# First-layer value products issued in three bursts of four, four and five token tiles in a two-layer cross-attention kernel

## What is computed

```python
q = _split_heads(hidden_states @ w_q, HEADS)
k = _split_heads(text @ w_k, HEADS)
v = _split_heads(text @ w_v, HEADS)
out_text = _merge_heads(_sdpa(q, k, v))            # softmax(q k^T / sqrt(dh)) v, 1593 text tokens
out_ip = _merge_heads(_sdpa(q, k_ip, v_ip, mask=mask_ip))   # 8 further tokens
out = (out_text + IP_SCALE * out_ip) @ w_out + b_out + residual
```

## Time and profile before

| What | Value |
|---|---|
| Median of 3 runs | 1550.36 us |
| The profiled execution: its own time | 1552.15 us |
| The profiled execution: span of the trace | 1550.2 us |
| TensorE busy | 1456.7 us (94%) |
| VectorE busy | 1119.9 us (72%) |
| ScalarE busy | 1060.8 us (68%) |
| First layer's products (line 1083), first and last start | 230.3 us, 636.4 us |
| First layer's products: MATMUL records, busy | 2080, 175.5 us |

### The profile page before, as it was taken

How to read it: one execution, slowest core, us unless ns; L and a number is a source line. 1 busy time by engine, 2 the same in 40 slices (tenths; PEclk the granted TensorE clock), 3 DMA queues, 4 the chain that set the end, 5 groups by cost and what they waited for, 6 DMA issues and landing times. The chain is left out here.

```text
span 1550.2 us, 32737 instructions
## 1 busy us (share of the span) xinstructions
PE 1456.7 (94%) x12886; PEld 911.9 (59%) x12886; DVE 1119.9 (72%) x1572; ACT 1060.8 (68%) x1962; POOL 188.8 (12%) x363
## 2 busy tenths in 40 slices
PE   6797959999999999999999999999999999999995
PEld 4454513333333333477777777777777777777774
DVE  5777768887787877876767777777777777777625
ACT  2454538877877877767767777777777777777752
POOL 4653300000101101000010000000000000000000
PEclk9899959999999999899999999999999999999996
DMA  5266851221221212110011101100011001100000
GB/s 158 75 161 174 226 115 48 53 51 40 58 54 47 66 40 51 42 26 23 17 26 30 29 19 26 26 23 20 23 26 26 22 18 27 26 23 16 7 1 17
DMA packets 82902, 75.89 MB, mean 49 GB/s; under 512 B 28608, under 2 KB 70964, under 8 KB 82756
## 3 DMA queue, kind: packets, MB, share of 16 engines
q1 hardware_dynamic: 82756, 73.88, 18.3%
HBM read 47.73 MB, written 26.09 MB: 48 GB/s over the span
## 5 line engine op out<-in xcount | busy, mean ns | idle before, releaser
L1364 DVE TENSOR_TENSOR whole<-late,whole 128x1024 f16<-128x1024 f32 (+1 forms) x280 | 320.1, 1143 | 99.3 <-ACT whole L1223 96.2
L1349 DVE TENSOR_REDUCE mx<-ps_y 128x2 f32<-128x800 f32 (+2 forms) x227 | 223.9, 986 | 106.1 <-PE ps_y L1030 105.4
L1107 PE MATMUL ps_v<-eh,whole 128*128 128x269 f16 x1040 | 293.1, 282 | 0.0
L1107 PE MATMUL ps_n<-eh,whole 128*128 128x269 f16 x1040 | 291.6, 280 | 0.0
L1223 ACT CAST whole<-late 128x1024 f16<-128x1024 f32 (+1 forms) x280 | 275.6, 984 | 8.9
L1109 PE MATMUL ps_v<-el,whole 128*128 128x269 f16 x960 | 269.1, 280 | 0.0
L1110 PE MATMUL ps_v<-eh,whole 128*128 128x269 f16 x960 | 269.1, 280 | 0.0
L1110 PE MATMUL ps_n<-eh,whole 128*128 128x269 f16 x960 | 268.2, 279 | 0.0
L1109 PE MATMUL ps_n<-el,whole 128*128 128x269 f16 x960 | 268.1, 279 | 0.0
L1349 DVE TENSOR_REDUCE mx<-ps_x 128x2 f32<-128x800 f32 (+2 forms) x198 | 195.3, 987 | 82.0 <-PE ps_x L1030 81.1
L1349 DVE TENSOR_REDUCE mx<-ps_t 128x2 f32<-128x800 f32 (+2 forms) x215 | 211.4, 983 | 32.8 <-PE ps_t L1030 31.9
(11 more groups left out here) (433 smaller groups left out, 2072.9 us busy)
## 6 DMA issues: line engine op xcount, KB each, us to landing
e<-in_ctx SPq DMA_DIRECT2D x4, 1536.0 KB
kb<-k_parts SPq DMA_DIRECT2D x80, 74.9 KB
kb<-k_parts SPq DMA_DIRECT2D x80, 74.7 KB
k_parts<-kp SPq DMA_DIRECT2D x12, 400.0 KB
vb<-v_cols SPq DMA_DIRECT2D x40, 117.0 KB, 2.1
v_cols<-late SPq DMA_DIRECT2D x4, 1040.0 KB, 11.7
late<-v_cols SPq DMA_DIRECT2D x40, 104.0 KB, 2.0
qb<-q_parts SPq DMA_DIRECT2D x160, 25.0 KB
```

The lines of the kernel that those rows point to most:

```text
L1107: pe.matmul(ps, hi, eh, start=(t == 0), stop=False)
L1349: nc.vector.tensor_reduce(mx[:, pair % 2, c, :], bank("max", pair, c)[:, :, 0:w], AX.X, ALU.max).then_inc(chunk_max, 1)
L1364: nc.vector.tensor_tensor(pl[s % 2][:, t0:t0 + w, :], ring[:, turn % EXPS, 0:w], ph[s % 2][:, t0:t0 + w, :], ALU.subtract).then_inc(low_do ...
```

## The change

The table puts the same 13 token tiles behind three fills: four behind fill 1, four behind fill 5 and five behind fill 9. The loop in `products` takes them two at a time, so that inside a burst the order of tiles and heads is the one of before. Each wait, each operand and the number of matmuls stay.

```diff
-PRODUCTS_AFTER = {1: (0, 1), 3: (2, 3), 5: (4, 5), 7: (6, 7), 9: (8, 9), 11: (10, 11), 13: (12,)}
+PRODUCTS_AFTER = {1: (0, 1, 2, 3), 5: (4, 5, 6, 7), 9: (8, 9, 10, 11, 12)}
...
-                    for i in range(2):
-                        for t in tiles:
-                            r0 = 32 * (2 * i + t % 2)
-                            last = pe.matmul(ps_v[r0:r0 + W0, 0:S], vb0[:, n, t, i, :], pe32[:, n, t, i * S:(i + 1) * S],
-                                             start=(t < 2), stop=(t >= NT - 2))
+                    for t0 in tiles[::2]:
+                        for i in range(2):
+                            for t in range(t0, min(t0 + 2, NT)):
+                                r0 = 32 * (2 * i + t % 2)
+                                last = pe.matmul(ps_v[r0:r0 + W0, 0:S], vb0[:, n, t, i, :], pe32[:, n, t, i * S:(i + 1) * S],
+                                                 start=(t < 2), stop=(t >= NT - 2))
```

## The result

The change made the kernel slower by 6.5%: 1647.38 us (median of 4 runs, 1646.84 to 1656.37) against 1550.68 us, a ratio of 1.0648 with a 95% interval of 1.0629 to 1.0668. That is +97 us where +47 was forecast, and outside the range given (1583 to 1614 us).

What follows compares the result with a forecast made beforehand. It took TensorE and the round of three banks as both near the limit. 39 steps at +1.31 us (51 us) less 4 us hidden by stages gave +47 us on 1552.15, and 1597 us for the runs' median; range 1583 to 1614 us.

Steps and rivals of the forecast that it cites:

- What bounds the pair at full clock: First-layer pair: TensorE and the round of three banks are both close to the limit; a plain pair takes 9.29 us.
- the hops of three banks: A fill needs the bank of the fill three places before: 0.44 us to ScalarE, 1.02 reading, 0.06 release.
- The walk's places: Start times followed through one changed first-layer pair from the burst behind fill 9: 10.60 us, +1.31 us a pair.
- The price of a joined burst: First-layer bursts: four tiles 1.00 us and five tiles 1.44 us up to the next fill, estimated from 0.22 us passes.
- The chain's sum: 39 plain steps at +1.31 us, 51 us, less 0.2 us for each of 21 stages, 4 us: 47 us.
- Rival 1 (joins save): TensorE's own work bounds first-layer pairs; joins save 0.78 us a pair, 31 us in all, giving 1519 us; chance 0.06.
- rival 2: The clock falls in the first layer, on top of the forecast; four stretches of 3 us give 1609 us; chance 0.18.
- The 13 us taken for a pair wholly at the lower clock: In the clock case, TensorE's 8.1 us in a first-layer pair would become 13 or more, against 10.60.
- stages fill the gap in 21 steps: Argument against the clock falling: stage work fills TensorE's gap between the third burst and the next first one.
- some more stretches: Further first-layer low-clock stretches beyond the four assumed, one reason given for the range's upper end of 1614 us.
- the upper price of the joined bursts: First-layer joined bursts costing as much as those they replace: 0.48 us more a pair, 19 us in 40.
- The signs named beforehand: First layer: copies 10.6 us apart, fills 5, 9, 13 waiting 0.5 to 1.3 us; clock below 1.00 shows its fall.

Runs made afterwards that it cites:

- e1_busy12: The change plus six extra matmuls, results unused, behind fill 12 in steps 2 to 39: 1600.85 us, ratio 1.0328.
- the last experiment: Two tables against the changed kernel, putting products where TensorE waits for a bank: 1535.11 us and 1528.18 us.
- e8_busy12_two: The change plus two extra matmuls, results unused, behind fill 12 in each pair: 1632.5 us, ratio 1.0515.
- e7_spread_b: The changed kernel with bursts 2, 2, 2, 2, 4, 1 behind fills 1, 3, 7, 9, 12, 14: 1528.18 us, 0.9864 of the kernel before.

## Why the prediction was wrong in its size

- **What bounds the pair at full clock** was right: the hops of three banks, with 0.44 us to the reader, 1.02 us of reading and 0.06 us of release. The walk's places lie within 0.07 us of the trace. The hop into `turn_max` was left out; it did not bind here, but it cost a quarter of a microsecond a pair in two of the runs above.
- **The price of a joined burst** was right: 0.98 us measured against 1.00, and 1.30 up to `turn_max` against 1.32.
- **The chain's sum** was right: 45 us measured (e1_busy12) against 47. Ten pairs grew by 11.63 us, where 10 x 1.31 - 7 x 0.2 = 11.7. That it fits so closely is partly luck: a plain pair grew by 1.25 us and not 1.31, and a stage hid 0.12 us ((10 x 1.25 - 11.63) / 7) and not 0.2, and the two misses cancel.
- **Rival 1 (joins save)** lost: a join does save TensorE time, which becomes idle time. The Trainium skill ("TensorEngine Tiling (Array Packing)", Tiling Modes) says that a change of the tiling mode drains the engine. The rows agree that something is saved: four tiles joined take 0.98 us up to the next fill, two bursts of two 2 x 0.56. No run here separates the change of mode from the rest of that difference. Of the two tables of the last experiment the first keeps two joins and the second one, where they do no harm.
- **The step that failed is what the clock costs.** The sum has no term for it; the prediction kept it as rival 2, at four stretches of 3 us each and a chance of 0.18. It came, on top of the forecast: 24 stretches, 150 us low, 52 us lost. Three things in rival 2 were wrong. First, the number was chosen, not worked out: four stretches had no row behind them, although the same sentence found the new gap emptier (2.3 of 3.5 us; the trace has 2.08 of 3.71) than the one stretch ahead of a fall in the trace (2.45 of 3.40 us). Its own comparison spoke for more than 0.18. Second, the price: 3 us was put on a stretch of 13.7 us, and three such stretches, in pairs with stages, cost 5.2 to 5.4 us each. The pair with 10.2 us of low clock took 14.34 us in place of 10.54. The 13 us taken for a pair wholly at the lower clock were TensorE's busy time alone; but the bursts stand in the chain, and they stretch from 1.05 to 1.90 and from 1.48 to 2.74 us. Third, "stages fill the gap in 21 steps" was wrong: the mean clock of the nine plain pairs ahead of the first stage is 0.93, that of the seven with stages behind them 0.82.

```profile
237.50:337.20 99.70, 79.60 (x918) 32.61 (x918) 70.10 (x82) 67.86 (x100) 4.97 (x27) 0.93 0.17 45
337.20:433.30 96.10, 79.66 (x762) 33.58 (x762) 58.42 (x70) 55.37 (x88) 6.80 (x26) 0.82 0.15 38
```

- **The range** went up to 1614 us with "some more stretches"; twenty more weren't meant by that. It is also narrower than its own terms: the upper price of the joined bursts (19 us) alone gives 1616.
- **The signs named beforehand** told the cases apart: the copies are 10.54 us apart in plain pairs, and the clock is below 1.00 between 240 and 620 us. TensorE waits 0.58 us for fill 5 and 1.12 us for fill 13. Fill 9 starts 0.06 us behind the exponentials of fill 6, as walked, but TensorE is idle for 0.08 us only and not for 0.5 or more, since `turn_result` and fills 7 and 8 stand in that wait.

Not settled: what decides which of the 40 pairs fall into a low stretch. It differs from kernel to kernel, in the rows above the same 3.40 us stood twice without a fall and then with one, and the times spread where the clock falls often (the runs of e8_busy12_two over 18 us, those of e7_spread_b over 3 us).

## What to carry to other kernels

Where a few banks go round between TensorE and its readers, work that is free to move belongs where TensorE waits for a bank anyway; a burst ahead of a fill whose reader is idle goes onto the path with its whole length, whatever the join saves on TensorE. Walk one period from fill to reader to fill with the trace's own intervals, and write down every instruction that waits for a bank, also the small ones (`turn_max` here). Then look at the emptiest stretch of TensorE that the new order has: if it is emptier than one behind which the trace shows the clock falling, put a term for the fall into the sum, and price it with the chain walked again at the lower clock. How often it comes can't be read from one such stretch: here it came in some pairs and not in others.

## What the runs showed of the hardware

The clock fell to 1.2 GHz with no long pause on TensorE: it fell 24 times, and the longest idle time in the 40 pairs is 1.17 us. Ahead of the fall at 281.2 us, 3.40 us had 1.76 us of work. Extra matmuls whose results nobody uses kept the clock up: with six in each pair, 0.83 us of work, the low clock went from 150 to 27 us and the kernel ran 46 us faster. A microsecond at the lower clock cost 0.35 us here (52 for 150). And the time at the lower clock doesn't add up over edits: the last join alone has 38 us of it and the first two alone 7 us, and all together 150 us.
